# Down projection in two column halves, contraction outermost over eight token tiles, weight rings on GpSimd's queue

## The chip, the cores and the metric

The kernel runs on one core of one Trainium2 chip. The metric is the device time of one execution in microseconds (us). The core has a matrix engine (TensorE; PE in the trace, with its weight loads as PEld), VectorE (DVE), ScalarE (ACT), GpSimd (POOL) and a queue engine, SyncE (SP), each with its own stream of instructions; they meet at semaphores. DMAs are issued from an engine's queue and run on 16 shared DMA engines.

## The reference

One transformer block with adaptive layer norm over 2048 tokens of width 1024; the change lies in its last matrix product, the down projection of a quantised feed-forward part.

```python
x = x + ga * attention(layernorm(x) * (1 + ca) + sa)      # x1
h = layernorm(x) * (1 + cb) + sb
xf = h / 128.0
inter   = silu(xf @ w_gate.T) * (xf @ w_up.T)             # 2048 x 2752
inter_q = trunc(clip(inter * 128.0, -128, 127)).astype(int8)
down    = inter_q.astype(float32) @ w_down.T              # 2048 x 1024, contraction over 2752
out     = trunc(clip(down * 128.0, -128, 127)).astype(int8)
x = x + gb * out
```

`gb` is one gate value per column.

## The kernel before, in words

The kernel is a row of stages (modulation and QKV, attention, output projection, gate/up, down), each a block of five instruction streams with a barrier between blocks. Only the end of gate/up and the stage down are touched.

**Sizes.** A contraction tile is 128 of the 2752 rows; there are 22 (`IT`), the last with 64 rows (`LASTI`). There are 16 token tiles (`TT`) of 128 tokens. `QW` is 256 columns, a quarter of 1024; `NB` is 512. Each weight is split into a high part and a remainder (`w_hi`, `w_lo`, both float32r), so each product costs two matmuls, with the int8 intermediate (made float32r) as the loaded operand and the weights as the streamed one.

**Gate/up (L1093).** For each of 22 row tiles and four blocks of 512 tokens, 24 matmuls for the gate and 24 for up (L1257), streamed 512 wide. GpSimd's queue stores the int8 result to DRAM (L1140), SyncE's the last tile's. When the matmuls of tile 20 are done, SyncE loads the first quarter of the down weights into `shared[0]` (L1165).

**Down (L1273).** Four quarters of 256 columns; in each the 16 token tiles in order, in each tile 22 contraction tiles by two matmuls (L1461), 44 in all, into one of two PSUM banks. That is 64 steps. ScalarE converts the next tile's int8 operand (L1381, L1382), multiplies the finished sum by 128 (L1394) and takes magnitude and sign (L1396, L1397). VectorE clips (L1432), rounds (L1435), truncates (L1081 to L1083), applies the gate (L1437) and adds x1 (L1440). SyncE stores the part and loads the x1 part two tiles on. Order on ScalarE in a step: the next operand, this sum, this magnitude, so the next operand but one stands behind a wait for VectorE's clip.

**Weights.** The first quarter is split by ScalarE and VectorE at the start of the stage (L1402, L1423); the other three by GpSimd, one quarter ahead, into the second pair of buffers (L1368 and L1372), after SyncE has loaded them (L1269, L1270). The intermediate is fetched after the barrier by nine DMAs in blocks of 512 tokens (L1332 to L1335), the first split in two so that tile 0 can start early (L1405, L1408, L1409). Most steps run in hardware loops (`Fori`) with a body of two steps.

## Time and profile before

| | us |
|---|---|
| median of three runs (range) | 3878.38 (3876.57 to 3881.32) |
| the profiled execution | 3881.62 |
| its span | 3879.9 |
| PE busy | 3690.1 (95%) |
| DVE busy | 2415.0 (62%) |
| ACT busy | 1732.0 (45%) |
| POOL busy | 1627.1 (42%) |
| first and last start of a down matmul | 3457.3 and 3873.2 |

The span runs from the first to the last instruction, and the profiled execution is 1.7 us longer than it. Busy shares are averages over stages with different limits. A busy PE is not a PE at its peak: the records of pipelined matmuls overlap, so what a matmul costs is read from the distance between two starts. `PEclk` is the granted TensorE clock as a share of full speed (2.4 GHz).

### The profile page before, as it was taken

The numbers are of one execution on the slowest core, as the hardware profiler recorded it, in microseconds if no ns is written. First come the engines' busy times: TensorE is split into PE (matmuls) and PEld (weight loads), VectorE is DVE, ScalarE is ACT, GpSimd is POOL, SyncE is SP. The second block draws the span as 40 slices with busy tenths as digits, with TensorE's granted clock in tenths as the row PEclk, the third lists the DMA queues.
The fourth block names the chain that finished last, engine by engine and source line by source line (L and its number), as shares of the span: only waits on it lengthen the run. The fifth ranks groups of instructions, "written<-read, shape, count | busy, mean of one in ns | idle before, by whom it ended". The sixth has DMA issues, their size and how long they took to land. (4 is left out here: it accounts for less than half of the span.)

```text
span 3879.9 us, 59156 instructions
## 1 busy us (share of the span) xinstructions
PE 3690.1 (95%) x19372; PEld 2401.0 (62%) x19372; DVE 2415.0 (62%) x4160; ACT 1732.0 (45%) x3071; POOL 1627.1 (42%) x549
## 2 busy tenths in 40 slices
PE   6998999999999999999999979799999999979889
PEld 4776444444444444444444358688888888868888
DVE  6433787777787777777777558544444444445554
ACT  3110466665666656666666633222222222125555
POOL 1111587787787777788788820000000000001110
PEclk8998899999999999999999999899999999999999
DMA  6654100101001010100100035711011111042121
GB/s 226 184 180 133 34 12 23 34 15 32 23 15 31 23 24 23 34 15 20 34 23 4 9 106 181 205 28 28 28 31 35 28 28 27 17 132 70 45 64 45
DMA packets 186866, 218.32 MB, mean 56 GB/s; under 512 B 29268, under 2 KB 148820, under 8 KB 182808
## 3 DMA queue, kind: packets, MB, share of 16 engines
q1 hardware_dynamic: 168488, 153.92, 14.3%
q0 software_dynamic: 15856, 59.52, 4.8%
q8 instruction: 121, 1.98, 0.2%
q10 hardware_dynamic: 2304, 2.10, 0.2%
q14 instruction: 97, 0.79, 0.1%
HBM read 152.70 MB, written 62.27 MB: 55 GB/s over the span
## 5 line engine op out<-in xcount | busy, mean ns | idle before, releaser
L689 DVE TENSOR_REDUCE att_chunk_max<-att_scores 128x1 f32<-128x512 f32 x2048 | 1284.7, 677 | 411.4 <-PE att_scores L760 404.2
L675 ACT ACTIVATE att_exp<-att_scores_T 128x512 f32<-128x512 f32 x2048 | 1122.3, 595 | 734.6 <-PE att_scores_T L774 716.3
L646 POOL TENSOR_TENSOR att_exp_pair<-att_exp 128x2048 f32<-128x2048 f32 x256 | 1169.5, 4579 | 440.7 <-ACT att_exp L675 440.7
L774 PE MATMUL att_scores_T<-att_q_stack,att_k_stack 98*128 98x512 f32 x2048 | 863.0, 424 | 13.1 <-ACT att_exp L675 9.6
L760 PE MATMUL att_scores<-att_k_stack,att_q_stack 96*128 96x512 f32 x2048 | 798.4, 436 | 40.2 <-DVE att_chunk_max L689 27.2
L774 PEld LDWEIGHTS att_scores_T<-att_q_stack,att_k_stack 98*128 98x128 f32 x2048 | 386.4, 189 | 497.8 <-ACT att_exp L675 290.4
L785 PE MATMUL att_y_acc<-att_exp,att_v_head 128*32 128x512 f32 x4096 | 547.9, 607 | 0.9 <-ACT att_exp L675 0.9
L760 PEld LDWEIGHTS att_scores<-att_k_stack,att_q_stack 96*128 96x128 f32 x2048 | 395.9, 193 | 245.2 <-DVE att_chunk_max L689 185.3
L1461 PE MATMUL down_acc<-dn_wd_hi,h_hi 128*128 128x256 f32 (+1 forms) x1408 | 369.8, 299 | 52.3 <-ACT h_hi L1382 37.1
L1140 POOL DMA_DIRECT2D inter_scratch<-gu_inter x84 | 45.2, 538 | 884.1 <-DVE gu_inter L1083 884.1
L1461 PE MATMUL down_acc<-dn_wd_lo,h_hi 128*128 128x256 f32 (+1 forms) x1408 | 355.2, 289 | 0.0
L1461 PEld LDWEIGHTS down_acc<-dn_wd_hi,h_hi 128*128 128x128 f32 (+1 forms) x1408 | 279.2, 198 | 70.8 <-ACT h_hi L1382 38.9
L655 POOL TENSOR_TENSOR att_exp_pair<-att_exp_pair 128x2048 f32<-128x2048 f32 x64 | 293.5, 4587 | 5.0
L1192 ACT ACTIVATE gu_magnitude<-gu_value 128x512 f32<-128x512 f32 x88 | 55.7, 633 | 516.7 <-DVE gu_value L1223 516.7
L1461 PEld LDWEIGHTS down_acc<-dn_wd_lo,h_hi 128*128 128x128 f32 (+1 forms) x1408 | 279.8, 199 | 0.0
L1222 DVE TENSOR_TENSOR gu_rounded<-gu_up_acc,gu_rounded 128x512 f32<-128x512 f32 x88 | 60.9, 692 | 323.7 <-PE gu_up_acc L1257 323.7
L1257 PE MATMUL gu_gate_acc<-h_hi,shared_split 128*128 128x512 f32 x704 | 225.6, 392 | 13.4 <-DVE shared_split L1209 13.4
L1257 PE MATMUL gu_up_acc<-h_hi,shared_split 128*128 128x512 f32 x704 | 223.8, 389 | 0.0
L799 PE MATMUL att_den_acc<-att_exp_pair,att_ones 128*32 128x512 f32 x1536 | 201.8, 597 | 3.5 <-POOL att_exp_pair L646 3.4
L785 PEld LDWEIGHTS att_y_acc<-att_exp,att_v_head 128*32 128x32 f32 x4096 | 80.7, 108 | 184.6 <-issue 176.2
L1050 PE MATMUL wo_wo_acc<-wo_wo_hi,shared_split 128*128 128x512 f32 x512 | 164.0, 396 | 13.9 <-DVE shared_split L990 13.4
L708 DVE RECIPROCAL att_den_acc<-att_den_acc 128x64 f32<-128x64 f32 x256 | 140.2, 553 | 58.6 <-PE att_den_acc L799 58.6
(185 smaller groups left out, 4749.1 us busy)
## 6 DMA issues: line engine op xcount, KB each, us to landing
att_q_stack<-q_scratch SPq DMA_DIRECT2D x96, 256.0 KB, 4.9
shared_raw<-in_wd_t SPq DMA_DIRECT2D x4, 2688.0 KB, 10.4
qkv_x_tile<-in_x SPq DMA_DIRECT2D x16, 512.0 KB, 4.8
q_scratch<-qkv_qk_out_hi POOLq DMA_DIRECT2D x32, 256.0 KB, 3.2
q_scratch<-qkv_qk_out_lo POOLq DMA_DIRECT2D x32, 256.0 KB, 4.2
qkv_wqkv_raw<-in_wmod POOLq DMA_DIRECT2D x8, 1024.0 KB, 7.6
qkv_wmod<-in_wmod POOLq DMA_DIRECT2D x8, 1024.0 KB, 8.2
y_scratch<-att_y_out SPq DMA_DIRECT2D x32, 256.0 KB, 2.4
```

The source lines that it names most:

```text
L646: nc.gpsimd.tensor_tensor(ps[PAIR_SLOT[j]][:], pr[2 * j % NP][:], pr[(2 * j + 1) % NP][:], ALU.add).then_inc(pair_done, 1)
L655: nc.gpsimd.tensor_tensor(first[:], first[:], ps[PAIR_SLOT[j]][:], ALU.add).then_inc(quad_done, 1)
L675: nc.scalar.activation(pr[k % NP][:, h * NB:(h + 1) * NB], stp[bank(GH * k + h)][:], ACT.Exp, scale=INV_SQRT_DH).then_inc(exp_done, 1)
L689: nc.vector.reduce_max(cmax[c % 2][:, q:q + 1], turn_buffer(u, q)[:], AX.X).then_inc(sm_done, 1)
L708: nc.vector.reciprocal(dp[:, cols], dp[:, cols]).then_inc(rden_done, 1)
L760: nc.tensor.matmul(turn_buffer(u, q)[:], qs[c % 4][0:SR, h, qt * P:(qt + 1) * P], ks[c // QB % 2][0:SR, kc * NB:(kc + 1) * NB], start=True ...
L774: nc.tensor.matmul(stp[bank(i)][:], ks[c // QB % 2][0:SR + 2, k * P:(k + 1) * P], qs[c % 4][0:SR + 2, h, :], start=True, stop=True).then_i ...
L785: ins = nc.tensor.matmul(yp[h * DH:(h + 1) * DH, :], vg[c // QB % 2][:, k, :], pr[k % NP][:, h * NB:(h + 1) * NB], start=(k == 0), stop=(k ...
L799: ins = nc.tensor.matmul(dp[h * DH:(h + 1) * DH, :], ones[:], part[:, h * NB:(h + 1) * NB], start=(i == 0), stop=(i == ND - 1))
L1050: ins = nc.tensor.matmul(acc[j][:, half * NB:(half + 1) * NB], ysp[j][a][:, k, :], w[z][:, k, half * NB:(half + 1) * NB], start=(k == 0 an ...
L1257: ins = nc.tensor.matmul(bank[n % 2][:], w[j][a][:, m * HALF_W + k * P:m * HALF_W + (k + 1) * P], h2[z], start=(k == 0 and q == 0), stop=( ...
L1461: ins = nc.tensor.matmul(acc[j][:, 0:QW], lhs[j][rows, k, :], w[q % 2][n][rows, k, :], start=(k == 0 and n == 0), stop=(k == IT - 1 and n ...
```

## The change

The stage down is written anew. It now works on two halves of 512 columns. In each half, phase A runs over token tiles 0 to 7 with the contraction outermost: for each of the 22 contraction tiles, eight token tiles by two matmuls, into eight PSUM banks. Phase B then runs tiles 8 to 15 one after another, 44 matmuls each, as before but 512 wide. Hardware loops are gone; everything is written out.

Weights have one pair of buffers instead of two. Contraction tiles 0 to 7 of the first half are loaded in gate/up, along with the first four of the intermediate (`load_first_inter`); all other tiles come one by one through a ring of four slots, by DMAs on GpSimd's queue, and are split by ScalarE (`weights_hi`) and VectorE (`weights_lo`). GpSimd computes nothing. The rest of the intermediate comes in four DMAs by contraction tile, with whole rows of 2048 tokens. In the second half the weights are written over those of the first while TensorE works on the first half's last tile (`w_used`). The elementwise work is 512 wide, in the order of `posts`; x1 has three buffers, and the sum is formed in them.

```diff
             sp.wait_ge(u_acc, 1 + QB * (IT - 1))
-            load_down(sp, shared[0], wd_t, 0, down_loaded)
+            load_down(sp, shared[0], wd_t, down_loaded)
+            sp.wait_ge(out_stored, 16 * QB * (IT - 1))
+            load_first_inter(sp, shared[0], inter_dram, down_loaded)
             store_inter(sp, IT - 1, True)
             sp.wait_ge(last_stored, 16 * QB)
...
+DN_PRE = 8
+DN_FIRST = 4
+def load_down(sp, raw, wd_t, loaded):
+    sp.dma_start(raw[:, 0:DN_PRE * DN_W].rearrange("p (k n) -> p k n", n=DN_W),
+                 wd_t[0:DN_PRE * P, 0:DN_W].rearrange("(k p) n -> p k n", p=P)).then_inc(loaded, 16)
+def first_inter(raw):
+    return raw[:, DN_PRE * DN_W:DN_PRE * DN_W + DN_FIRST * T // 4].bitcast(I8).rearrange("p (k t) -> p k t", t=T)
+def load_first_inter(sp, raw, inter_dram, loaded):
+    sp.dma_start(first_inter(raw), inter_dram[0:DN_FIRST].rearrange("k p t -> p k t")).then_inc(loaded, 16)
...
         inter = sb("inter_all", [P, IT, T], I8)
-        wraw = shared_raw[:, 0:IT * QW].rearrange("p (k n) -> p k n", n=QW)
-        w = [[sb(f"wd_{n}{i}", [P, IT, QW], F32R) for n in ("hi", "lo")] for i in range(2)]
+        first = first_inter(shared_raw)
+        raw = shared_raw[:, 0:(RING + GT) * W].rearrange("p (k n) -> p k n", n=W)
+        w = [sb(f"wd_{n}", [P, IT, W], F32R) for n in ("hi", "lo")]
         room = lhs_room[:].rearrange("p k t -> p (k t)")
-        lhs = [room[:, i * IT * P:(i + 1) * IT * P].rearrange("p (k t) -> p k t", t=P) for i in range(2)]
+        lhs_b = [room[:, i * IT * P:(i + 1) * IT * P].rearrange("p (k t) -> p k t", t=P) for i in range(2)]
+        lhs_a = [room[:, 2 * IT * P + i * HALF_T:2 * IT * P + (i + 1) * HALF_T] for i in range(2)]
...
+        def posts(h):
+            first = [[(h, 0), (h, 1)]]
+            mid = [[(h, i + 1), (h, GT + i - 1)] for i in range(1, GT - 1)]
+            return first + mid + [[(h, TT - 2)], [(h, TT - 1)]]
...
+            for s in range(NPOST):
+                toks, cols = x_part(s)
+                sp.wait_ge(o_done, s + 1)
+                sp.dma_start(out[0, toks, cols], xt[s % NXB][:]).then_inc(o_stored[s % NXB], 16)
+                if s + NXB < NPOST:
+                    sp.wait_ge(o_stored[s % NXB], 16 * (s // NXB + 1))
+                    load_x(s + NXB)
...
+            def load_w(h, k):
+                r = rows(k)
+                pool.dma_start(raw_of(h, k)[r], wd_t[k * P:k * P + r.stop, h * W:(h + 1) * W]
+                               ).then_inc(ring_loaded[slot(h, k)], 16)
+            for k in range(DN_PRE, IT):
+                pool.wait_ge(w_split, k - DN_PRE + 1 if k < DN_PRE + RING else k - RING + 1)
+                load_w(0, k)
+                if k == DN_PRE:
+                    pool.dma_start(gate[:], mod_dram[5 * D:6 * D].rearrange("(a d) -> a d", a=1).broadcast_to([P, D])
+                                   ).then_inc(g_loaded, 16)
+            for k in range(IT):
+                pool.wait_ge(w_split, IT if k < RING else IT + k - RING + 1)
+                load_w(1, k)
...
+            def weights_hi(h, k):
+                if h == 0 and k < DN_PRE:
+                    if k == 0:
+                        act.wait_ge(down_loaded, 32)
+                else:
+                    act.wait_ge(ring_loaded[slot(h, k)], nth_load(h, k))
+                if h:
+                    act.wait_ge(w_used, k + 1)
+                nc.scalar.copy(w[0][rows(k), k, :], raw_of(h, k)[rows(k)]).then_inc(w_hi, 1)
+            def slice_a(h, k):
+                for i, ks in enumerate(GROUPS):
+                    if h == 0 and k == ks.start and k >= DN_FIRST:
+                        act.wait_ge(i_loaded[i], 16)
+                src = first if h == 0 and k < DN_FIRST else inter
+                n = h * IT + k
+                if n >= 2:
+                    act.wait_ge(a_used, n - 1)
+                nc.scalar.copy(lhs_a[n % 2][rows(k)], src[rows(k), k, 0:HALF_T]).then_inc(a_done, 1)
+            def tile_b(h, i):
+                if h == 0 and i == 0:
+                    act.wait_ge(i_loaded[len(GROUPS) - 1], 16)
+                if h * GT + i >= 2:
+                    act.wait_ge(acc_done, h * TT + GT + i - 1 if i >= 2 else (h - 1) * TT + TT - 1 + i)
+                cols = slice((GT + i) * P, (GT + i + 1) * P)
+                nc.scalar.copy(lhs_b[i % 2][:, 0:FULL, :], inter[:, 0:FULL, cols])
+                nc.scalar.copy(lhs_b[i % 2][0:LASTI, FULL, :], inter[0:LASTI, FULL, cols]).then_inc(b_done, 1)
+            def evacuate(h, t):
+                act.wait_ge(acc_done, h * TT + t + 1)
+                if h or t >= GT:
+                    s = ORDER.index((h, t - GT) if t >= GT else (h - 1, t + GT))
+                    act.wait_ge(o_done, s + 1)
+                nc.scalar.mul(evac(t), acc[t % GT][:], 128.0).then_inc(evac_done, 1)
+            def magnitude(s):
+                val = evac(ORDER[s][1])
+                act.wait_ge(clipped, s + 1)
+                if s >= 2:
+                    act.wait_ge(o_done, s - 1)
+                nc.scalar.activation(mag[s % 2], val, ACT.Abs)
+                nc.scalar.activation(sgn[s % 2], val, ACT.Sign).then_inc(parts_done, 1)
+            s = 0
+            for h in range(NH):
+                for k in range(IT):
+                    if h == 0:
+                        weights_hi(0, k)
+                    elif k + RING < IT:
+                        weights_hi(1, k + RING)
+                    if h == 0 or k >= 2:
+                        slice_a(h, k)
+                    if h and k == 3:
+                        magnitude(s)
+                        s += 1
+                    if k == IT - 3:
+                        tile_b(h, 0)
+                for t in range(GT):
+                    evacuate(h, t)
+                steps = posts(h)
+                for i in range(GT):
+                    for _ in steps[i]:
+                        magnitude(s)
+                        s += 1
+                    if i + 1 < GT:
+                        tile_b(h, i + 1)
+                    if h == 0 and i == GT - 1:
+                        slice_a(1, 0)
+                        slice_a(1, 1)
+                        for k in range(RING):
+                            weights_hi(1, k)
+                    evacuate(h, GT + i)
+            magnitude(s)
...
+            def clip(s):
+                h, t = ORDER[s]
+                v.wait_ge(evac_done, h * TT + t + 1)
+                nc.vector.tensor_scalar(evac(t), evac(t), 127.0, -128.0, ALU.min, ALU.max).then_inc(clipped, 1)
+            def post(s):
+                h, t = ORDER[s]
+                val, m = evac(t), mag[s % 2]
                 v.wait_ge(parts_done, s + 1)
+                ln.link(nc.vector.tensor_scalar(val, m, RNE, -RNE, ALU.add, ALU.add))
+                ln.link(trunc_tail(nc, v, ln, val, val, m, sgn[s % 2], m))
+                ln.link(nc.vector.tensor_tensor(val, val, gate[:, h * W:(h + 1) * W], ALU.mult))
+                v.wait_ge(x_loaded[s % NXB], 16 * (s // NXB + 1))
+                nc.vector.tensor_tensor(xt[s % NXB][:], xt[s % NXB][:], val, ALU.add).then_inc(o_done, 1)
                 v.wait_ge(o_done, s + 1)
...
+            for k in range(IT):
+                weights_lo(0, k)
+                if k == 10:
+                    v.wait_ge(g_loaded, 16)
+                    gate_of(nc, ln, gate, gwork)
+            s = 0
+            for h in range(NH):
+                for i, step in enumerate(posts(h)):
+                    if h == 0 and i == GT:
+                        for k in range(RING):
+                            weights_lo(1, k)
+                    for n in range(len(step)):
+                        clip(s + n)
+                    if h == 0 and i == GT:
+                        for k in range(RING, RING + 3):
+                            weights_lo(1, k)
+                    for _ in step:
+                        post(s)
+                        s += 1
+                    if h == 0 and i == GT:
+                        for k in range(RING + 3, IT):
+                            weights_lo(1, k)
...
+            for h in range(NH):
                 for k in range(IT):
...
+                    pe.wait_ge(w_split, h * IT + k + 1)
+                    pe.wait_ge(a_done, h * IT + k + 1)
+                    for t in range(GT):
+                        if k == 0 and h:
+                            pe.wait_ge(evac_done, (h - 1) * TT + GT + t + 1)
+                        for n in range(2):
+                            ins = nc.tensor.matmul(acc[t][:], lhs_a[(h * IT + k) % 2][rows(k), t * P:(t + 1) * P],
+                                                   w[n][rows(k), k, :], start=(k == 0 and n == 0),
+                                                   stop=(k == IT - 1 and n == 1))
+                        if k == IT - 1:
+                            ins.then_inc(acc_done, 1)
+                    if k < IT - 1:
+                        ins.then_inc(a_used, 1)
+                    else:
+                        pe.sem_inc(a_used, 1)
+                for i in range(GT):
+                    pe.wait_ge(b_done, h * GT + i + 1)
+                    pe.wait_ge(evac_done, h * TT + i + 1)
+                    for k in range(IT):
+                        for n in range(2):
+                            ins = nc.tensor.matmul(acc[i][:], lhs_b[i % 2][rows(k), k, :], w[n][rows(k), k, :],
+                                                   start=(k == 0 and n == 0), stop=(k == IT - 1 and n == 1))
+                        if h == 0 and i == GT - 1 and k < IT - 1:
+                            ins.then_inc(w_used, 1)
+                    ins.then_inc(acc_done, 1)
+                    if h == 0 and i == GT - 1:
+                        pe.wait_ge(acc_done, TT)
+                        pe.sem_inc(w_used, 1)
```

TensorE at the start of the stage down; `down_acc0` and so on are PSUM banks. Before:

```order
L1461 MATMUL down_acc0<-dn_wd_hi0,h2_hi0 128x256
L1461 MATMUL down_acc0<-dn_wd_lo0,h2_hi0 128x256
L1461 MATMUL down_acc0<-dn_wd_hi0,h2_hi0 128x256
L1461 MATMUL down_acc0<-dn_wd_lo0,h2_hi0 128x256
L1461 MATMUL down_acc0<-dn_wd_hi0,h2_hi0 128x256
```

Now:

```order
L1544 MATMUL down_acc0<-dn_wd_hi,h2_hi0 128x512
L1544 MATMUL down_acc0<-dn_wd_lo,h2_hi0 128x512
L1544 MATMUL down_acc1<-dn_wd_hi,h2_hi0 128x512
L1544 MATMUL down_acc1<-dn_wd_lo,h2_hi0 128x512
L1544 MATMUL down_acc2<-dn_wd_hi,h2_hi0 128x512
```

Twice the columns for each loaded operand, and the bank changes with every second matmul.

GpSimd in the stage down, before (the last four rows stand there three times):

```order
L1361 DMA dn_gate_b<-mod_scratch 128x1024
L1368 CAST dn_wd_hi<-shared_raw 128x5376
L1368 CAST dn_wd_hi<-shared_raw 64x256
L1372 TENSOR_TENSOR dn_wd_lo<-shared_raw,dn_wd_hi 128x5376
L1372 TENSOR_TENSOR dn_wd_lo<-shared_raw,dn_wd_hi 64x256
```

Now:

```order
L1395 DMA shared_raw<-in_wd_t 128x512
L1402 DMA dn_gate_b<-mod_scratch 128x1024
L1395 DMA shared_raw<-in_wd_t 128x512 x12
L1395 DMA shared_raw<-in_wd_t 64x512
L1395 DMA shared_raw<-in_wd_t 128x512 x21
L1395 DMA shared_raw<-in_wd_t 64x512
```

The twelve computing instructions are gone, and 36 weight DMAs have come, 14 in the first half and 22 in the second.

ScalarE around the end of the first half, now (L1418 is `weights_hi`, L1428 `slice_a`, L1445 `evacuate`, L1452 and L1453 `magnitude`):

```order
L1452 ACTIVATE dn_work<-shared_raw 128x512
L1453 ACTIVATE dn_work<-shared_raw 128x512
L1428 CAST h_hi<-dn_inter_all 128x1024 x2
L1418 CAST dn_wd_hi<-shared_raw 128x512 x4
L1445 ACTIVATE shared_raw<-down_acc 128x512
L1418 CAST dn_wd_hi<-shared_raw 128x512 x3
L1428 CAST h_hi<-dn_inter_all 128x1024
L1418 CAST dn_wd_hi<-shared_raw 128x512
L1428 CAST h_hi<-dn_inter_all 128x1024
L1452 ACTIVATE dn_work<-shared_raw 128x512
```

The second half's first two slices and first four weight tiles stand ahead of the evacuation of the first half's last tile.

## Rows read from the trace of the kernel before

**Rows 1.** Windows, five stretches: busy us (instructions) by engine, granted clock, DMA share

```profile
core 0: us, PE busy (x) PEld busy (x) DVE busy (x) ACT busy (x) POOL busy (x), PEclk, DMA share, GB/s
2900.00:3100.00 200.00, 200.00 (x884) 165.60 (x883) 91.26 (x142) 44.72 (x68) 9.68 (x18) 1.00 0.12 32
3457.30:3873.50 416.20, 377.46 (x2816) 359.22 (x2816) 224.46 (x450) 231.98 (x321) 52.74 (x12) 0.94 0.24 72
...
3478.00:3510.00 32.00, 17.27 (x109) 16.26 (x109) 23.59 (x23) 10.80 (x16) 17.58 (x4) 0.77 0.27 83
...
3457.20:3459.20 2.00, 1.89 (x9) 1.89 (x10) 0.96 (x1) 1.00 (x2) 0.00 (x0) 0.50 1.14 312
3459.20:3461.20 2.00, 2.00 (x11) 2.00 (x11) 0.26 (x1) 0.00 (x0) 0.00 (x0) 0.50 1.15 287
3461.20:3463.20 2.00, 1.08 (x8) 0.88 (x8) 0.00 (x0) 1.77 (x3) 0.00 (x0) 0.93 1.14 284
```

**Rows 2.** Timeline, PE, end of one down tile (start, duration in us)

```profile
3560.33 0.28 PE L1461 MATMUL down_acc<-dn_wd_hi,h_hi 128*128 128x256 f32 x1
3560.45 0.28 PE L1461 MATMUL down_acc<-dn_wd_lo,h_hi 128*128 128x256 f32 x1
3560.66 0.38 PE L1461 MATMUL down_acc<-dn_wd_hi,h_hi 64*128 64x256 f32 x1
3561.09 0.38 PE L1461 MATMUL down_acc<-dn_wd_hi,h_hi 128*128 128x256 f32 x1
...
3566.74 0.38 PE L1461 MATMUL down_acc<-dn_wd_hi,h_hi 128*128 128x256 f32 x1
```

**Rows 3.** Timeline, PE, the first and the last of 24 gate/up matmuls

```profile
3427.25 0.39 PE L1257 MATMUL gu_up_acc<-h_hi,gu_w_hi 128*128 128x512 f32 x1
3432.46 0.39 PE L1257 MATMUL gu_up_acc<-h_hi,gu_w_lo 128*128 128x512 f32 x1
```

**Rows 4.** Timeline, around GpSimd's first weight split, by engine

```profile
3484.78 5.20 POOL L1368 CAST dn_wd_hi<-shared_raw 128x5376 fp32r<-128x5376 f32 x2 [32.77 <-DMA shared_raw<-in_wd_t]
3490.07 12.38 POOL L1372 TENSOR_TENSOR dn_wd_lo<-shared_raw,dn_wd_hi 128x5376 fp32r<-128x5376 f32 x2
...
3490.92 10.95 DVE L1435 TENSOR_SCALAR dn_rounded<-dn_magnitude 128x256 f32<-128x256 f32 x1 [0.79 <-ACT dn_sign L1397]
...
3505.02 0.42 ACT L1396 ACTIVATE dn_magnitude<-dn_value 128x256 f32<-128x256 f32 x1 [11.33 <-DVE dn_value L1432]
```

**Rows 5.** Timeline, from the barrier to the first down matmul, by engine

```profile
3451.05 2.94 ACT L1402 CAST dn_wd_hi<-shared_raw 128x1024 fp32r<-128x1024 f32 x3 [4.88 <-PEq L1098]
3455.89 1.36 ACT L1405 CAST h_hi<-dn_inter_all 128x1408 fp32r<-128x1408 int8 x1 [1.91 <-DMA dn_inter_all<-inter_scratch]
...
3457.31 0.58 PE L1461 MATMUL down_acc<-dn_wd_hi,h_hi 128*128 128x256 f32 x1 [13.58 <-ACT h_hi L1405]
```

**Rows 6.** Groups by form, from 3350 us on: mean ns of one after the comma

```profile
L1381 ACT CAST h_hi<-dn_inter_all 128x2688 fp32r x54 | 130.7, 2421 | 0.0
L1192 ACT ACTIVATE gu_magnitude<-gu_value 128x512 f32<-128x512 f32 x9 | 5.7, 632 | 54.8 <-DVE gu_value L1223 54.8
L1082 DVE TENSOR_TENSOR gu_rounded<-gu_rounded,gu_value 128x512 f32<-128x512 f32 x10 | 6.9, 692 | 0.3
L1226 DVE TENSOR_SCALAR gu_rounded<-gu_magnitude 128x512 f32<-128x512 f32 x9 | 3.8, 427 | 11.0 <-ACT gu_sign L1193 11.0
```

**Rows 7.** DMA issues, whole span: count, KB, median us to landing

```profile
q_scratch<-qkv_qk_out_lo POOLq DMA_DIRECT2D x32, 256.0 KB, 4.2
...
qkv_wqkv_raw<-in_wmod POOLq DMA_DIRECT2D x8, 1024.0 KB, 7.6
```

**Rows 8.** Timeline, the end, by engine

```profile
3873.23 0.28 PE L1461 MATMUL down_acc<-dn_wd_lo,h_hi 64*128 64x256 f32 x1
...
3873.55 0.38 ACT L1394 ACTIVATE dn_down<-down_acc 128x256 f32<-128x256 f32 x1 [4.18 <-PE down_acc L1461]
...
3877.21 0.43 DVE L1440 TENSOR_TENSOR dn_out_part<-dn_x_part,dn_rounded 128x256 f32<-128x256 f32 x1
```

More of the change, by code:

```diff
@@ L1302, in stage_down @@
-        dve = sem("down_dve_links")
-        LINKS = 5
-        full = slice(0, IT - 1)
-        PARTS = [(slice(0, P), slice(k, min(k + 4, IT - 1))) for k in range(0, IT - 1, 4)]
-        EARLY, LATE = slice(0, IT // 2), slice(IT // 2, IT - 1)
-        PARTS.append((slice(0, LASTI), slice(IT - 1, IT)))
-        block = st.enter_context(nc.Block())
-        def steps(eng, step, before=None):
-            for q in range(NQ):
-                if before:
-                    before(q)
-                first = 2 if q == 0 else 0
-                for t in range(first):
-                    step(t, t, t, 0, q)
-                with eng.Fori(0, (TT - 2 - first) // 2) as i:
-                    for j in range(2):
-                        step(i * 2 + (q * TT + j + first), i * 2 + (j + first), j, i + (q * TT + first) // 2, q)
-                for t in range(TT - 2, TT):
-                    step(q * TT + t, t, t % 2, (q * TT + t) // 2, q)
+        work = sb("work", [P, 4, W])
@@ new lines, in stage_down, with rows, evac @@
+        dve = sem("down_dve_links")
+        block = st.enter_context(nc.Block())
+        def rows(k):
+            return slice(0, LASTI) if k == IT - 1 else slice(0, P)
+        def evac(t):
+            return raw[:, RING + t % GT, :]
+        def posts(h):
+            first = [[(h, 0), (h, 1)]]
+            mid = [[(h, i + 1), (h, GT + i - 1)] for i in range(1, GT - 1)]
+            return first + mid + [[(h, TT - 2)], [(h, TT - 1)]]
+        ORDER = [one for h in range(NH) for step in posts(h) for one in step]
@@ new lines, in x_part, with slot, nth_load, raw_of @@
+        def x_part(s):
+            h, t = ORDER[s]
+            return slice(t * P, (t + 1) * P), slice(h * W, (h + 1) * W)
+        def slot(h, k):
+            return (k - DN_PRE) % RING if h == 0 else k % RING
+        def nth_load(h, k):
+            order = [(0, i) for i in range(DN_PRE, IT)] + [(1, i) for i in range(IT)]
+            mine = [one for one in order if slot(*one) == slot(h, k)]
+            return 16 * (mine.index((h, k)) + 1)
+        def raw_of(h, k):
+            return raw[:, k, :] if h == 0 and k < DN_PRE else raw[:, slot(h, k), :]
@@ L1356, in _, with load_inter, load_x @@
-            steps(sp, step, before)
-            sp.wait_ge(o_stored, 16 + 16 * NQ * TT)
+            def load_inter(i):
+                ks = GROUPS[i]
+                r = rows(ks.start)
+                sp.dma_start(inter[r, ks, :], inter_dram[ks, r, :].rearrange("k p t -> p k t")).then_inc(i_loaded[i], 16)
+            def load_x(s):
+                toks, cols = x_part(s)
+                sp.dma_start(xt[s % NXB][:], x1_dram[toks, cols]).then_inc(x_loaded[s % NXB], 16)
+            for i in range(len(GROUPS)):
+                load_inter(i)
@@ L1410, in _ @@
-            steps(act, step)
+            def weights_hi(h, k):
[16 more added lines that the diff above has]
+                nc.scalar.copy(lhs_a[n % 2][rows(k)], src[rows(k), k, 0:HALF_T]).then_inc(a_done, 1)
@@ L1465, in _ @@
-            steps(pe, step, before=lambda q: q and pe.wait_ge(w_split, len(PARTS) + q))
+            for h in range(NH):
+                for k in range(IT):
+                    pe.wait_ge(w_split, h * IT + k + 1)
[26 more added lines that the diff above has]
+                        pe.sem_inc(w_used, 1)
```

150 lines of the change are left out of this document (30 added, 120 removed).

## The prediction

> **What bounds the kernel now.** I read the table of windows first: it says which stretches TensorE fills. In gate/up it is busy without a break at full clock; in the stage down (3457.3 to 3873.5 us) it does 2816 matmuls in 416.2 us at a mean clock of 0.94 [rows 1]. Then the timeline of TensorE inside down, for its undisturbed pace. Starts are 0.12 us apart. The last contraction tile has 64 rows, and on the way into it and out of it two starts are 0.2 us apart or more; a whole tile takes 5.65 us (3561.09 to 3566.74) where 44 x 0.12 gives 5.28, so 0.37 us per tile goes there [rows 2]. 64 tiles at 5.65 are 361.6 us. The other 54.5 of the 416.1 us between the first start and the end of the last matmul are the slow start and three disturbances.
>
> The disturbances show on the timelines of the other engines. While GpSimd subtracts (12.38 us), VectorE's rounding of 256 columns takes 10.95 us, where 512 columns take 0.43 in gate/up [rows 6]; ScalarE waits 11.33 us for the clip behind it, and the operand of a later tile stands behind that on ScalarE [rows 4]. TensorE is busy 17.27 of 32 us in that window and the clock falls to 0.77 [rows 1]. It happens three times, once per quarter that GpSimd splits. Last, the start: ScalarE begins at 3451.05, waits for the intermediate until 3455.89, and TensorE starts at 3457.31 [rows 5], at half clock (0.50, which is 1.2 GHz) for about 3.9 us, after 13.6 us without work [rows 1, 5].
>
> **TensorE's own time.** The change makes 2816 matmuls of 256 columns into 1408 of 512. The nearest rows are gate/up's: same stationary size, same type, 512 wide. From the first to the last of 24 it is 5.21 us for 23 distances [rows 3], 0.2265 us each; 884 in 200 us say the same [rows 1]. 1408 x 0.2265 = 318.9 us. The 64-row tile comes once per phase A (for all eight tiles in a row) and once per tile of phase B: 2 x (1 + 8) = 18 times instead of 64. At 0.37 us, 6.7 us; together 325.6 against 361.6, a gain of 36.0 us. Bounds for the price of one passage at 512 wide: nothing (it hides) and 0.8 us (twice), so -7 to +8 us; I take the measured 0.37.
>
> The Trainium skill ("TensorE: Matmul & The Clock Gate", the section on sustained throughput) gives about 131 ns for a 512-wide matmul in a sustained stream; by it the matmuls would need an estimated 184 us. This trace has 226 ns for the same width, so I leave it out of the sum.
>
> **Start.** ScalarE still begins at 3451.05: the barrier hangs on gate/up's last store, which does not move, and the two early loads are issued some 40 us before. SyncE's new wait for GpSimd's stores stands ahead of its own first store of the last row tile; those two stores carry neighbouring blocks of 48 matmuls, so they lie 48 x 0.2265 = 10.9 us apart, far more than a small store needs, and nothing queues. ScalarE needs one weight tile of 512 (about 0.6 us: a 512-wide ACT pass is 632 ns [rows 6]) and a slice of 1024 (about 1.0 us: three of that size took 2.94 [rows 5]); VectorE's remainder lies beside the slice. TensorE starts at about 3452.8, 4.5 us earlier. Bounds: 3452.2, and 3456.3 if the start pays a DMA wait as before. I keep the 3.9 us at half clock: 1.95 us lost.
>
> **The splits and slices in phase A.** TensorE needs 16 x 0.2265 = 3.62 us per contraction tile. ScalarE needs 0.6 + 1.0, VectorE 0.7 [rows 6]. Both are hidden. The slices have two buffers, so slice k starts when TensorE leaves k - 2 and is ready 2.6 us before it is needed; the 2.7 us for tile 8's operand before slice 20 and VectorE's 4.7 us for the gate after weight tile 10 fit too. The intermediate's tiles 4 to 9 (1.5 MB) are needed 11 us after the start; at the 287 to 312 GB/s of that stretch [rows 1] they need 5 to 6.
>
> **The ring.** A weight DMA of 256 KB is issued when its slot's last user has been split, four contraction tiles ahead, 14.5 us. GpSimd's queue landed 256 KB in 4.2 us and 1024 KB in 7.6 [rows 7]. I take 4.2, which hides. The Trainium skill ("SBUF — State Buffer", on DVE blocking DMA) says that a DMA issued by GpSimd waits for its descriptors while VectorE runs an op in a two-port mode. That speaks against this edit. Such ops (the clips and roundings) last 0.43 us here [rows 6]; by the rule a load would come an estimated 0.5 to 1 us later, inside ten us of slack, and the sum stays. Seen the other way, rows 4 are such a blockade by GpSimd's arithmetic, which is what goes.
>
> **Phase B.** A tile takes TensorE 44 x 0.2265 + 0.37 = 10.34 us. ScalarE: evacuation 0.6, two magnitudes and signs 2.4, the next operand 2.7 (2421 ns and the short one [rows 6]): 5.7, hidden. VectorE is the tight one: per post one rounding (0.46 with its gap) and five two-operand ops at 0.73 (692 ns and the gap) make 4.1, or 4.4 if I allow 0.3 for waits between; two posts, 8.2 to 8.8. Ahead of them stand the evacuation (done 0.9 after the tile's last start: 0.32 to its start [rows 8] and 0.6) and the first magnitude (1.2), which VectorE waits for. So 10.3 to 10.9 us against 10.34: VectorE keeps up or falls back up to 0.6 us per tile, over six steps at most 3 us. The next operand waits behind the magnitudes and has 4 us to spare. At the half's end the second half's first remainder is due about 7.6 us into the last tile, 2.7 us early, less that lag. I take nothing; bounds 0 and 4 us.
>
> **Between the halves.** ScalarE splits four weight tiles during the last tile, done 7.2 us into it; TensorE also waits for its own last matmul (some 0.3 us). I take 0.3. The three quarter boundaries with GpSimd go altogether. x1 parts: a store and a load of 256 KB, at 4.2 us each at most [rows 7], against three posts of 4 us or more: hidden.
>
> **End.** Last start 3873.23, evacuation at 3873.55, last add at 3877.21, span end 3879.9 [rows 8]. Twice the width adds 0.2 (evacuation), 0.1 (clip), 0.4 (magnitude, sign), 0.1 (rounding), 5 x 0.27 and about 0.5 for a store twice as large: 2.7 us.
>
> **Sum.** TensorE's stretch: 325.6 + 1.95 + 0.3 = 327.9 instead of 416.1, -88.2; start -4.5; end +2.7: -90.0. The span becomes 3789.9; the profiled execution 3881.6 - 90.0 = 3791.6. That execution was 3.2 us above the median of three, so 3788.4, say 3788.
>
> **Rivals.**
> 1. VectorE bounds phase B. Against: 8.8 us of posts in 10.34. For: no cover is left, and its ops rewrite the buffer that they read. If a step takes 12 us, six steps lose 1.66 each less 4 of slack in each half, some 12 us, and the second half's first weights come late, 5 more: 3805.
> 2. The wider matmul brings nothing, because weight load and stream do not overlap as in gate/up: 0.24 us each, twice today's. 1408 x 0.0135 = +19 us: 3807. Rows 3 speak against it. The GpSimd stalls would still go.
> 3. The early fetch does nothing, or half a buffer is short at the change of halves: one stall of 4 to 10 us, with the clock at half for 3.9 us again: 3792 to 3800.
> 4. Slower than before: the ring bounds. Four loads in flight serve one contraction tile per (L + 1.5)/4 us, L being issue to landing. Up to L = 13 us it is free; 36 tiles come this way, and 90 us are gone when each costs 2.5 us more, at L = 23 us. The longest nearby rows are 7.6 us for four times the size. With L = 25 it would be 3788 + 36 x 3.0 = 3896.
>
> **How the numbers follow.** Forecast 0.80, rival 1 0.07, rival 2 0.04, rival 3 0.06, rival 4 0.03. Own range of the forecast: -7 (passages hide), +8 (passages twice), start +3.5, phase B +4, not all at once: 3780 to 3800. To hold 8 in 10 with rivals 1 and 3 in part: 3779 to 3804. About 0.2% (8 us) is what a measurement here can tell from no change. Everything but rival 4 is far beyond it: faster 0.96, same 0.01, slower 0.03.
>
> **What would show it.** First down matmul near 3452.8 us; starts 0.2265 apart; phase B tiles 10.3 us; no VectorE op above 1.5 us in the stage; no gap in TensorE above 1 us at the change of halves and a clock of 1.00 after the first 4 us; last matmul near 3780. Wrong would be: TensorE idle for ScalarE's operand in phase B (rival 1), starts 0.24 apart (2), ScalarE waiting for a ring load longer than a us or two (4).

## The result, and the profile after

The changed kernel takes 3792.88 us (median of four, 3792.38 to 3793.74), the kernel before 3878.45 (3876.57 to 3881.32). The ratio is 0.9779, 95% interval 0.9763 to 0.9794: 85.6 us faster. The forecast was 3788, range 3779 to 3804, so the measured time lies 4.9 us above the forecast and inside the range.

The chain of work that ended last, for the stage down (start, length in us):

```profile
3451.56 82.88 PE down_acc L1544 x352
3534.44 83.21 PE down_acc L1558 x352
3617.66 0.29 issue
3617.95 80.30 PE down_acc L1544 x352
3698.24 83.22 PE down_acc L1558 x352
3781.48 0.61 ACT shared_raw L1445
...
3787.19 0.69 DVE dn_x_part L1508
```

The whole stage is four unbroken runs of 352 matmuls: phase A and phase B of each half, with 0.29 us between the halves. From then on one elementwise chain runs to the end of the span at 3790.4. In the kernel before, the chain runs off TensorE up to 3508.31 and again for 40 us around each of the other two splits (3572.51 to 3612.45, 3677.39 to 3718.10): through SyncE's queue and a store of the output, then VectorE's rounding of 10.95 us as in [rows 4], then ScalarE.

The table of windows, at the start and later (columns as in [rows 1]), and the start on ScalarE and TensorE:

```profile
3452.00:3454.00 2.00, 2.00 (x6) 1.52 (x6) 1.23 (x2) 1.40 (x2) 1.11 (x3) 0.50 0.98 349
3454.00:3456.00 2.00, 2.00 (x7) 1.52 (x6) 0.13 (x1) 0.00 (x0) 0.54 (x1) 0.50 1.00 379
3456.00:3458.00 2.00, 2.00 (x8) 1.63 (x7) 0.00 (x0) 0.00 (x0) 0.00 (x0) 0.74 1.06 407
...
3640.00:3695.00 55.00, 55.00 (x243) 45.27 (x243) 6.93 (x10) 23.44 (x27) 3.22 (x6) 1.00 0.10 32
```

```profile
3449.85 0.62 ACT L1418 CAST dn_wd_hi<-shared_raw 128x512 fp32r<-128x512 f32 x1 [4.89 <-PEq L1098]
3450.38 1.04 ACT L1428 CAST h_hi<-shared_raw 128x1024 fp32r<-128x1024 int8 x1
...
3451.56 0.77 PE L1544 MATMUL down_acc<-dn_wd_hi,h_hi 128*128 128x512 f32 x1 [9.04 <-ACT h_hi L1428]
```

ScalarE no longer waits for the intermediate (against [rows 5]); TensorE starts 1.71 us after it. The half clock is still there and ends inside the window 3456 to 3458 (mean 0.74). The first 13 distances between TensorE's starts take 5.59 us (3451.56 to 3457.15) where 13 x 0.2265 is 2.94: 2.65 us are lost, which is 5.3 us at half clock. Beyond that the clock is 1.00 (against 0.94 over the stage in [rows 1]).

The end of one phase B tile on TensorE, and VectorE and ScalarE around one:

```profile
3543.57 0.39 PE L1558 MATMUL down_acc<-dn_wd_hi,h_hi 128*128 128x512 f32 x1
3543.80 0.39 PE L1558 MATMUL down_acc<-dn_wd_lo,h_hi 128*128 128x512 f32 x1
3544.11 0.49 PE L1558 MATMUL down_acc<-dn_wd_hi,h_hi 64*128 64x512 f32 x1
3544.45 0.39 PE L1558 MATMUL down_acc<-dn_wd_lo,h_hi 64*128 64x512 f32 x1
3544.77 0.50 PE L1558 MATMUL down_acc<-dn_wd_hi,h_hi 128*128 128x512 f32 x1
3545.11 0.40 PE L1558 MATMUL down_acc<-dn_wd_lo,h_hi 128*128 128x512 f32 x1
```

```profile
3565.14 0.43 DVE L1498 TENSOR_SCALAR shared_raw<-shared_raw 128x512 f32<-128x512 f32 x1
3566.31 0.43 DVE L1498 TENSOR_SCALAR shared_raw<-shared_raw 128x512 f32<-128x512 f32 x1 [0.75 <-ACT shared_raw L1445]
3567.35 0.43 DVE L1504 TENSOR_SCALAR shared_raw<-dn_work 128x512 f32<-128x512 f32 x1 [0.61 <-ACT dn_work L1453]
...
3575.54 0.43 DVE L1498 TENSOR_SCALAR shared_raw<-shared_raw 128x512 f32<-128x512 f32 x1
...
3570.59 0.29 ACT L1437 CAST h_hi<-dn_inter_all 64x128 fp32r<-64x128 int8 x1
3576.08 0.60 ACT L1445 ACTIVATE shared_raw<-down_acc 128x512 f32<-128x512 f32 x1 [5.20 <-PE down_acc L1558]
3576.57 0.62 ACT L1452 ACTIVATE dn_work<-shared_raw 128x512 f32<-128x512 f32 x1
```

Starts lie 0.23 us apart, and 0.31 to 0.34 at the four steps in and out of the 64-row tile: 0.40 us in all (0.37 at 256 wide, [rows 2]). A step of VectorE is 3565.14 to 3575.54, 10.40 us, the same as TensorE's tile (83.21 / 8): VectorE goes at TensorE's pace. Its clip of 3575.54 is done at 3575.97, and ScalarE takes the magnitude of it at 3576.57, right behind the evacuation; so VectorE has 0.6 us to spare per tile. ScalarE has the next operand at 3570.88 and then waits 5.20 us for TensorE. Together that is the 5.8 us by which VectorE may be late before TensorE waits; the expectations below use it.

### The profile page after: what moved, and what is told of

It is laid out like the page before. It is cut to its first block and busy times, and to the rows that moved or that the text cites. A ratio compares the mean times of both kernels' runs of the same rounds, so it can differ in the third digit from the quotient of the medians.

```text
span 3790.4 us, 54755 instructions
## 1 busy us (share of the span) xinstructions
PE 3642.6 (96%) x17964; PEld 2304.7 (61%) x17964; DVE 2357.0 (62%) x3973; ACT 1655.3 (44%) x2959; POOL 1594.9 (42%) x573
## 3 DMA queue, kind: packets, MB, share of 16 engines
q1 hardware_dynamic: 141368, 145.79, 13.6%
## 5 line engine op out<-in xcount | busy, mean ns | idle before, releaser
L774 PE MATMUL att_scores_T<-att_q_stack,att_k_stack 98*128 98x512 f32 x2048 | 863.3, 425 | 10.4 <-ACT att_exp L675 6.6
L1050 PE MATMUL wo_wo_acc<-wo_wo_hi,shared_split 128*128 128x512 f32 x512 | 163.9, 396 | 14.1 <-DVE shared_split L990 13.6
L1259 PEld LDWEIGHTS gu_gate_acc<-h_hi,shared_split 128*128 128x128 f32 x704 | 133.5, 190 | 41.7 <-issue 13.7
L1259 PEld LDWEIGHTS gu_up_acc<-h_hi,shared_split 128*128 128x128 f32 x704 | 132.0, 188 | 27.3
L1544 PE MATMUL down_acc<-dn_wd_hi,h_hi 128*128 128x512 f32 (+1 forms) x352 | 138.9, 395 | 9.3 <-ACT h_hi L1428 9.0
L1192 ACT ACTIVATE gu_sigmoid<-gu_gate_acc 128x512 f32<-128x512 f32 x88 | 52.7, 599 | 202.5 <-PE gu_gate_acc L1259 202.4
```

The source lines that it names most:

```text
L774: nc.tensor.matmul(stp[bank(i)][:], ks[c // QB % 2][0:SR + 2, k * P:(k + 1) * P], qs[c % 4][0:SR + 2, h, :], start=True, stop=True).then_i ...
L1050: ins = nc.tensor.matmul(acc[j][:, half * NB:(half + 1) * NB], ysp[j][a][:, k, :], w[z][:, k, half * NB:(half + 1) * NB], start=(k == 0 an ...
L1259: ins = nc.tensor.matmul(bank[n % 2][:], w[j][a][:, m * HALF_W + k * P:m * HALF_W + (k + 1) * P], h2[z], start=(k == 0 and q == 0), stop=( ...
L1544: ins = nc.tensor.matmul(acc[t][:], lhs_a[(h * IT + k) % 2][rows(k), t * P:(t + 1) * P], w[n][rows(k), k, :], start=(k == 0 and n == 0), s ...
```

## The experiments

Twelve runs, on three chips; the kernel before was timed beside each group, with medians of 3879.28 (e1 to e4), 3876.35 (e5 to e8) and 3882.69 us (e9 to e11, e8b). Single executions of it lie between 3873.5 and 3886.2. So differences of a few us between groups are read from ratios or from the stage's own stretch in the profile (first to last start of a down matmul; 329.5 us in the changed kernel, 415.9 in the one before).

### What the parts are worth

**e1: the width alone.**

```diff
-ins = nc.tensor.matmul(acc[t][:], ..., w[n][rows(k), k, :], start=(k == 0 and n == 0), ...)
+for c in (slice(0, W // 2), slice(W // 2, W)):
+    ins = nc.tensor.matmul(acc[t][:, c], ..., w[n][rows(k), k, c], start=(k == 0 and n == 0 and c.start == 0), ...)
```

> The changed kernel with each 512-wide matmul of the down stage issued as two of 256 columns (same bank, same operands, nothing else changed). Theory (the width is worth the fixed 13 ns that each matmul costs beyond its columns): 2816 starts of 0.120 us instead of 1408 of 0.2265, +19.0 us, less about 1 us because the 64-row passages are cheaper at 256 wide: about 3811 us against 3793. Rival (the gain came from the loop order, the buffers or the banks, not from the width): 3793 to 3797 us.

Measured: 3809.52 us (3806.86 to 3811.66), ratio 0.9821 (0.9808 to 0.9835), 17 us above the changed kernel. The stretch is 347.0 us (3451.2 to 3798.2), 17.5 more. The width is what the distances of 0.120 and 0.2265 us say it is; the rival falls.

**e2: the kernel before, GpSimd computes nothing.** Weights of the first quarter serve all four.

```diff
-ins = nc.gpsimd.tensor_copy(w[q % 2][0][rows, ks], wraw[rows, ks])
...
+pool.sem_inc(w_hi, 1)
...
-ins = nc.gpsimd.tensor_tensor(w[q % 2][1][rows, ks], ..., ALU.subtract)
...
+pool.sem_inc(w_split, 1)
...
-... w[q % 2][n][rows, k, :]
+... w[0][n][rows, k, :]
```

> The kernel before without GpSimd's arithmetic: the three later quarters are still loaded by SyncE, but not split; TensorE uses the first quarter's weights in all four, so the output's last three quarters are not the reference's. Theory (GpSimd's arithmetic blocks VectorE, and that is what stalls TensorE): the trace of before shows 144, 107 and 116 matmuls fewer than the undisturbed pace in the 40 us around each split, 367 x 0.1284 = 47 us, all of which goes: about 3831 us. Rival (the 2.7 MB load on SyncE's queue, ahead of the output stores and x1 loads, causes a good part): VectorE's add still waits 5 to 7 us for a store at each quarter, TensorE still idles there, and the time stays above 3845 us.

Measured: 3838.74 us (3838.16 to 3839.76), ratio 0.9896, 40.5 us below the kernel before. The stretch is 372.3 us, 43.6 less. The waits of this run (at the instruction <- what released it: us, times, longest):

```profile
DVE dn_out_part L1435 <- DMA out_dram<-dn_out_part: 9.2, 3, 5.1
PE down_acc L1456 <- ACT h_hi L1377: 4.9, 3, 2.9
```

Two windows of the same run (columns as in [rows 1]), each at one of the weight loads:

```profile
3480.00:3500.00 20.00, 16.36 (x117) 15.42 (x116) 8.21 (x22) 10.85 (x16) 0.00 (x0) 0.91 0.38 122
3560.00:3580.00 20.00, 20.00 (x160) 19.20 (x159) 10.18 (x27) 13.60 (x18) 0.00 (x0) 1.00 0.59 183
```

The add still waits for an output store behind the 2.7 MB load, three times, up to 5.1 us each; only at the first load (the window from 3480) does TensorE feel it. There 117 matmuls start in 20 us, where the undisturbed windows have 156 to 160: some 5 us. So the rival is right that the wait is there and wrong that it matters much: of the 47 us that I had counted in the three disturbances, GpSimd's arithmetic is 40 by the times (43.6 by the stretch), and the rest is about what is lost behind the first load. That this rest is the queue's is read from the wait for the store; no run takes the load off the queue.

**e3: the ring on SyncE's queue.**

```diff
-pool.dma_start(raw_of(h, k)[r], wd_t[...]).then_inc(ring_loaded[slot(h, k)], 16)
+sp.dma_start(raw_of(h, k)[r], wd_t[...]).then_inc(ring_loaded[slot(h, k)], 16)
```

> The changed kernel with the weight ring's and the gate's DMAs moved: the ring to SyncE's queue, between the intermediate's loads and the stores; the gate stays on GpSimd's. Theory (a ring load has some ten us of slack, whichever queue issues it): no change, 3791 to 3795 us. Rival (descriptor work on GpSimd costs VectorE or TensorE something): 2 us or more faster.

Measured: 3792.22 us (3791.09 to 3793.23), ratio 0.9777 against 0.9779. The queue makes no difference to the time. The 256 KB loads land in 2.7 us (median) from SyncE's queue and in 3.0 from GpSimd's in the changed kernel: 0.3 us, less than the 0.5 to 1 us of the estimate in the prediction, and inside the slack either way.

**e4: no early fetch of the intermediate.**

```diff
 load_down(sp, shared[0], wd_t, down_loaded)
-sp.wait_ge(out_stored, 16 * QB * (IT - 1))
-load_first_inter(sp, shared[0], inter_dram, down_loaded)
```

(the same call now stands first on SyncE in the stage down, and ScalarE's first slice waits for it)

> The changed kernel with the first four slices of the intermediate fetched after the barrier, into the same place, instead of in gate/up; weights early as they are. Theory: ScalarE's first slice waits for 1 MB issued at the barrier, about 5.5 us, so TensorE starts about 5 us later and everything behind it: about 3798 us. Rival (the early fetch does nothing, since the start is bound elsewhere): 3793 us.

Measured: 3797.20 us (3793.93 to 3799.52), ratio 0.9788 against 0.9779, so 3 to 4 us, at the limit of what these runs resolve. ScalarE's start in this run shows the wait itself:

```profile
3450.65 0.62 ACT L1417 CAST dn_wd_hi<-shared_raw 128x512 fp32r<-128x512 f32 x1 [4.88 <-PEq L1098]
3456.11 1.04 ACT L1429 CAST h_hi<-shared_raw 128x1024 fp32r<-128x1024 int8 x1 [4.84 <-DMA shared_raw<-inter_scratch]
```

The second instruction starts 5.46 us after the first, in the changed kernel 0.53: 4.9 us. Some 0.9 of them come back in this profile, because the half clock after the start costs 1.8 us here and not 2.65; the stretch is 328.6 us.

### What was said to be hidden, and how much cover it has

**e5: a longer VectorE step.**

```diff
+ln.link(nc.vector.tensor_tensor(m, m, sgn[s % 2], ALU.mult))   # twice, in each post
```

> The changed kernel with two more two-operand VectorE ops per post (they rewrite a scratch buffer that is not read again), 0.73 us each, 2.92 us per phase B step. Theory (VectorE's step needs 9.9 us when nothing holds it, against TensorE's 10.40, and a lag of 5.8 us is free because ScalarE has 5.2 us to spare for the next operand): the step becomes 12.8, the lag grows by 2.4 us a step, seven steps less 5.8 make about 11 us per half, and the second half's first remainder is late by about 3: +24, about 3817 us. Rival 1 (VectorE is hidden): 3793 to 3796. Rival 2 (VectorE bounds phase B already): 14 steps x 2.92, +41, about 3834.

Measured: 3825.63 us (3822.54 to 3826.17), ratio 0.9864: 33 us above the changed kernel. Between the two rivals, as the theory has it, but 9 us over its figure. The step is right. ScalarE's timeline at two magnitudes, one tile apart, and below it TensorE's waits in the stage:

```profile
3576.40 0.63 ACT L1452 ACTIVATE dn_work<-shared_raw 128x512 f32<-128x512 f32 x1 [7.10 <-DVE shared_raw L1498]
3589.14 0.63 ACT L1452 ACTIVATE dn_work<-shared_raw 128x512 f32<-128x512 f32 x1 [7.53 <-DVE shared_raw L1498]
```

```profile
PE down_acc L1560 <- ACT h_hi L1437: 14.8, 8, 2.3
PE down_acc L1546 <- DVE dn_wd_lo L1492: 5.0, 1, 5.0
```

ScalarE's first magnitude comes every 12.74 us (I had 12.8) and now waits for VectorE; less the 2.92 that were added, VectorE's own step is 9.82 us. TensorE waits eight times for the operand, 14.8 us, and 5.0 at the second half's first remainder. The stretch is 356.9 us, 27.4 more than in the changed kernel: 19.8 of waits, the rest half clock after them (mean 0.88 from 3600 to 3640, 0.97 from 3700 to 3811). The lag left at the end makes the tail 3.3 us longer, and the stage started 3 us later in this run, which is scatter. I had counted neither the clock nor the tail.

**e6: a ring of one.**

```diff
-RING = 4
+RING = 1
```

> The changed kernel with a ring of one slot instead of four. Theory (one weight tile per issue, landing 3.0, ScalarE's copy 0.6 and VectorE's remainder 0.7, about 5.0 us, against TensorE's 3.62): from tile 9 of the first half and tile 2 of the second on each tile costs 1.4 us more, about 13 and 26 us, 3 more for the post that stands among the remainders: +42, about 3835 us. Rival (weights land so early that the ring's depth does not matter): below 3800.

Measured: 3828.27 us (3826.92 to 3828.93), ratio 0.9873: 36 us above the changed kernel, the stretch 366.7, 37.2 more.

```profile
3504.24 0.62 ACT L1418 CAST dn_wd_hi<-shared_raw 128x512 fp32r<-128x512 f32 x1 [3.01 <-DMA shared_raw<-in_wd_t]
3508.79 0.62 ACT L1418 CAST dn_wd_hi<-shared_raw 128x512 fp32r<-128x512 f32 x1 [2.98 <-DMA shared_raw<-in_wd_t]
...
3505.88 0.54 POOL L1395 DMA_DIRECT2D shared_raw<-in_wd_t  x1 [4.04 <-DVE dn_wd_lo L1492]
```

One weight tile every 4.55 us, where I had 5.0: issue at 3505.88, ScalarE's copy at 3508.79, so 2.9 from issue to use. That is 0.93 us over TensorE's 3.62 a tile. Phase A of the first half is 8.5 us longer, which is nine tiles at 0.93. That of the second is 28.6 longer: some 20 tiles at 0.93 make 19, and the other 10 lie around the post that stands among the remainders, where TensorE waits 3.5 and 6.1 us and the clock falls after it (mean 0.89 from 3650 to 3680). Even a ring of one keeps more than half the gain.

**e8 and e8b: GpSimd's arithmetic back.** Two ops in each half's phase B, then four.

```diff
+if k in (RING - 1, IT - 1):
+    pool.wait_ge(acc_done, (TT if k == IT - 1 else 0) + GT + 3)
+    for n in range(2):                                              # e8b: range(4)
+        nc.gpsimd.tensor_tensor(busy, busy..., busy..., ALU.mult)   # e8b: ALU.subtract
...
```

> The changed kernel with two GpSimd tensor ops of 128 x 2560 added in each half's phase B (in place on a buffer that is free then), some 5.7 us each. Theory (they block VectorE for about 11 us, of which 5.8 are free): 5.5 us of TensorE's time per half, 1.6 for the second half's weights, up to 2 per half for the clock: 3806 to 3810 us, with VectorE ops of 5 us or more in the trace. Rival (the block was a matter of the old order, with ScalarE behind the clip): 3793 to 3796.

Measured: 3794.90 us (3793.10 to 3796.58), ratio 0.9786 against 0.9779: at most 3 us, where I had 13 to 17. By its number the rival was right; the ops themselves say otherwise (timeline of GpSimd and VectorE, then TensorE's wait for its operand in the whole stage):

```profile
3565.20 9.04 POOL L1411 TENSOR_TENSOR h_hi<-h_hi 128x2560 fp32r<-128x2560 f32 x2 [37.27 <-PE down_acc L1565]
...
3565.78 4.15 DVE L1505 TENSOR_SCALAR shared_raw<-shared_raw 128x512 f32<-128x512 f32 x1 [0.75 <-ACT shared_raw L1451]
3569.85 4.67 DVE L1511 TENSOR_SCALAR shared_raw<-dn_work 128x512 f32<-128x512 f32 x1
```

```profile
PE down_acc L1565 <- ACT h_hi L1443: 3.2, 2, 1.6
```

The blockade is there (4.15 and 4.67 us instead of 0.43), but a GpSimd op takes 4.5 us and not 5.7, so VectorE lost 8.0 us and not 11. With 5.8 us free that is 2.2 per half; TensorE waited 3.2 in all. I had scaled the length of GpSimd's op wrongly, from the subtraction of 5376 columns. (In the attention stage a GpSimd addition of 2048 columns takes 4.6 us. The op added here reads one buffer for both inputs; whether that makes it quicker was not tested.) Whether the free 5.8 us or the new order was the reason, this run could not say, hence the double dose.

> As e8, with four GpSimd ops in a row in each half instead of two (a subtraction in place of the product). Theory as it stands after e8 (an op of 128 x 2560 takes 4.5 us and VectorE stands for nearly all of it; a lag of 5.8 us is free): 18 us of VectorE less 5.8 free, about 11 us of TensorE per half, 2 to 4 more for the second half's weights and the end, the clock falls in the gap: 20 to 30 us above the changed kernel on the same chip. Rival (only the ops in a two-port mode are blocked, and the others run between): the additional two GpSimd ops cost less than 5 us.

Measured: 3817.76 us (3813.18 to 3819.96), ratio 0.9836; the changed kernel on the same chip (e11) 3794.46: +23.3. VectorE's timeline while GpSimd computes, and TensorE's wait:

```profile
3562.86 4.15 DVE L1505 TENSOR_SCALAR shared_raw<-shared_raw 128x512 f32<-128x512 f32 x1 [0.75 <-ACT shared_raw L1451]
3566.94 4.67 DVE L1511 TENSOR_SCALAR shared_raw<-dn_work 128x512 f32<-128x512 f32 x1
3571.65 4.83 DVE L1081 TENSOR_TENSOR dn_work<-shared_raw,dn_work 128x512 f32<-128x512 f32 x1
3576.51 4.82 DVE L1082 TENSOR_TENSOR shared_raw<-shared_raw,dn_work 128x512 f32<-128x512 f32 x1
```

```profile
PE down_acc L1565 <- ACT h_hi L1443: 19.7, 2, 9.9
```

Four VectorE ops in a row wait out four GpSimd ops, also the two that read two SBUF tensors (4.83 and 4.82 us instead of 0.69). VectorE loses 16.2 us, TensorE 9.9 per half: 16.2 less 5.8 is 10.4. These waits are 19.7 of the 23.3 us. So VectorE is as exposed to GpSimd's arithmetic in the new order as in the old one; what the new order has is a cushion of 5.8 us.

### The 64-row tile, and a faster version

**e7: zero rows in the changed kernel. e10: in the kernel before.**

```diff
+for part in (inter[LASTI:P, IT - 1, :], w[0][LASTI:P, IT - 1, :]..., w[1][LASTI:P, IT - 1, :]...):
+    nc.gpsimd.memset(part, 0.0).then_inc(padded, 1)
...
-... lhs_b[i % 2][rows(k), k, :], w[n][rows(k), k, :]
+... lhs_b[i % 2][:, k, :], w[n][:, k, :]
```

> The changed kernel with the last contraction tile filled up to 128 rows by zeros (three memsets by GpSimd at the start), so that every matmul uses 128 rows. Theory (the change between 128 and 64 rows costs 0.43 us per passage, 18 passages, not the 64-row matmul itself): -7.7 us, about 3785 us. Rival (the loss at a tile's end is the change of bank or a semaphore): no change, 3793 us.

Measured: 3786.02 us (3781.50 to 3786.68), ratio 0.9762; the stretch is 322.1 us, 7.4 less, 0.41 per passage.

> The kernel before with zero rows in its last contraction tile, so that every matmul uses 128 rows (five memsets by GpSimd at the start). Theory (a passage costs 0.37 us at 256 wide, 64 of them, of which a few lie where TensorE waits anyway): -22 us, about 3856 us. Rival (the loss at a tile's end is the change of tile): within 3 us of the kernel before.

Measured: 3863.14 us (3859.96 to 3865.00), ratio 0.9949 (0.9935 to 0.9963), 19.5 us below the kernel before. With 64 passages of 0.37 us it would be 23.7; TensorE's wait for its operand is longer in this run (42.0 us against 37.1 in the kernel before), so part of the gain went into waits. The loss at a tile's end is the change of row count, not the change of tile. The changed kernel's phase A says so too, where 16 matmuls with 64 rows stand in a row:

```profile
3530.18 0.39 PE L1544 MATMUL down_acc<-dn_wd_lo,h_hi 128*128 128x512 f32 x1
3530.50 0.49 PE L1544 MATMUL down_acc<-dn_wd_hi,h_hi 64*128 64x512 f32 x1
3530.84 0.39 PE L1544 MATMUL down_acc<-dn_wd_lo,h_hi 64*128 64x512 f32 x1
3531.07 0.39 PE L1544 MATMUL down_acc<-dn_wd_hi,h_hi 64*128 64x512 f32 x1
...
3534.06 0.39 PE L1544 MATMUL down_acc<-dn_wd_lo,h_hi 64*128 64x512 f32 x1
3534.37 0.50 PE L1558 MATMUL down_acc<-dn_wd_hi,h_hi 128*128 128x512 f32 x1
3534.71 0.40 PE L1558 MATMUL down_acc<-dn_wd_lo,h_hi 128*128 128x512 f32 x1
```

Two distances are long on the way in (0.32 and 0.34) and two on the way out (0.31 and 0.34); the 14 from 3530.84 to 3534.06 are 0.23 each.

**e9: zero rows, and TensorE kept busy between the stages.**

```diff
+for n in range(IDLE_MM):   # 30, in gate/up after the last tile
+    nc.tensor.matmul(gp[0][:], w[1][0][:, 0:P], h2_hi[0][:, 0, 0:NB], start=True, stop=True)
...
+for n in range(IDLE_DN):   # 7, at the start of the stage down
+    nc.tensor.matmul(acc[GT - 1][:], spare[:, 0:P], spare[:, 0:W], start=True, stop=True)
```

> The changed kernel with the zero rows, and with matmuls whose result nothing reads while TensorE would wait between the stages: 30 after gate/up's last (6.8 us) and 7 at the start of the stage down. Theory (the clock is at 1.2 GHz for the first 4.9 us of the stage because TensorE had nothing to do before): the granted clock is 1.00 from the first real matmul on, 2.4 us less than with zero rows alone: about 7.7 + 2.4 = 10 us below the changed kernel on the same chip. Rival (the two us between the two groups, or the barrier, let the clock fall anyway): no change against zero rows alone.

Measured: 3785.79 us (3784.55 to 3787.04), ratio 0.9752 (0.9739 to 0.9765); e11 on the same chip 3794.46 (3792.67 to 3796.75): 8.7 us less. The windows at the start, the second with the first real matmul (3453.98):

```profile
3450.00:3452.00 2.00, 1.73 (x8) 1.11 (x6) 0.02 (x1) 0.00 (x0) 0.00 (x0) 1.00 0.06 16
3452.00:3454.00 2.00, 1.71 (x8) 1.29 (x8) 0.69 (x1) 1.73 (x3) 1.75 (x2) 1.00 0.09 27
3454.00:3456.00 2.00, 2.00 (x10) 1.68 (x10) 0.84 (x2) 1.82 (x3) 2.00 (x5) 1.00 0.95 304
```

The clock stays at 1.00 over the barrier, and the stretch is 319.6 us: 1408 x 0.2265 is 318.9, so 0.7 us is left to gain in it at this number of matmuls. The stretch is 2.5 us shorter than in e7, by the profile, and in e7 the first 13 distances lost 2.6 us to the half clock (5.2 us of it, where the expectation has 4.9). The times alone do not show it: the ratios are 0.9752 here and 0.9762 in e7, on another chip, and their intervals overlap.

> The changed kernel again, on the chip of the three above. Both theories: within 2 us of its ratio of 0.978 to the kernel before; it says how much of a difference of a few us between chips and runs is nothing.

Measured: 3794.46 us, ratio 0.9774 (0.9760 to 0.9787), 0.0005 from the first.

## Why the prediction was right

**TensorE's stretch.** Predicted 327.9 us, measured 329.9 to the last matmul's end. The distance is 0.2265 to 0.227 us. A passage costs 0.40 and not 0.37 (18 of them: 0.5 us more), the half clock lasts 5.3 us and not 3.9 (0.7 more), the change of halves 0.29 (predicted 0.3); the last 0.8 us are spread over the phases. The half clock's length was taken over from the kernel before, and it is not a constant: read in the same way it is 5.3 us in this profile and 4.2 in e11, both after 9.0 us without work, 3.5 in e4 after 14.0, and 3.8 in the kernel before after 13.6.

**Start.** TensorE starts 1.71 us after ScalarE, predicted 1.75. That it started at 3451.56 and not at 3452.8 comes from ahead of the change: gate/up's last matmul began 1.2 us earlier than before. In e9's profile it lay 2.4 us later than in this one, and in the profiles of e8b and e11 the stage's first matmul starts at 3448.1 and 3455.7. This is scatter, and it was luck that it hid 1.2 of the 2 us by which the stretch was too long.

**Phase B.** VectorE kept up with 0.6 us to spare in 10.40: the forecast of 10.3 to 10.9 for its step reached over TensorE's own 10.34, and I took nothing for it. The step was sized wrong. I had put the evacuation ahead of the two posts, but the step's first clip works on a tile that was evacuated earlier, and only ScalarE's order of instructions sets its magnitude behind the evacuation. Left to itself VectorE needs 9.8 us (e5). So "I take nothing" came out for a better reason than mine. ScalarE's next operand had 5.2 us to spare, where I had 4. e5 shows what it would have been worth: 33 us for 2.92 us a step. This was the real risk of the change, and the cover of 5.8 us (0.6 and 5.2) is what made it small.

**End.** Predicted 2.7 us more, measured 2.6 (3781.1 to 3790.4, against 6.7 us).

**The rest.** Rival 1 fell by the trace and e5, rival 2 by the starts 0.2265 us apart and e1, rival 3 by the chain (0.29 us between halves) and e4, rival 4 by the trace, e3 and e6: a ring load lands in 3.0 us (median), where I took 4.2 and the rival needs more than 13, and ScalarE waits for one 1.1 us in all.

**What was off is the step from the profile to the median.** The sum gave 3791.6 for a profiled execution; the profiled one took 3792.38. I then took off 3.2 us, because the profiled execution before had been that much above the median of three. But executions of the kernel before scatter over 3873.5 to 3886.2 us, and the median of all of its runs moves by 6 us between chips, while the changed kernel's profiled execution was the fastest of its four. 3.2 of the 4.9 us by which 3788 was too low come from that correction.

**Where 86 us came from.** By experiments that undo or do one part: GpSimd's arithmetic 40.5 (e2), the width 17 (e1), fewer changes of row count about 12 (19.5 for all 64 before, by e10, less 7.4 for the 18 that are left, by e7), the early fetch 4 (e4). That is 74. Of the other 12, the kernel before lost 10.7 us of its stretch in e2 (372.3 less 64 x 5.65) at the start and behind the first load, of which 2.6 of half clock remain; 2.6 are paid at the end. Some 6 us are not assigned by the times; they are within the scatter of four differences. The stretches of the profiles close better. 86.4 us went: 43.6 with GpSimd's arithmetic (e2), 19.0 with the width by the two distances (17.5 measured in e1), and 16.5 with the passages at their prices (64 x 0.37 less 18 x 0.40; e10's time shows less because part of it went into waits). The last 7.3 are those 10.7 less 3.4 that the new stretch still loses in half clock, at the change of halves and spread over the phases.
